# A sorted edge sum by matmul: one-hots of 128 columns, or two halves of a group with 64 columns each

## What is computed

```python
xn  = layernorm(x)
e   = edge_attr_128 @ W_edge + b_edge              # [50000, 256]
msg = relu(xn[src] + e)
agg = segment_sum(msg, dst, 3125)                  # dst is sorted
h   = (1 + eps) * xn + agg
h   = relu(h @ W1 + b1) @ W2 + b2                  # then batch norm and relu
x   = x + h + linear_attention(xn)                 # 8 heads, elu + 1
x   = x + moe(layernorm(x))                        # 8 experts, top 2
```

## Time and profile before

| | us |
|---|---|
| median of 3 runs | 1186.91 |
| span of the profiled execution (the page gives no other total) | 1050.8 |
| TensorE busy | 964.7 (92%) |
| weight loads busy | 810.3 (77%) |
| VectorE busy | 671.7 (64%) |
| POOL busy | 555.1 (53%) |
| ScalarE busy | 513.5 (49%) |

### The profile page before, as it was taken

One profiled execution on the slowest core, in us unless ns is written; L12 is line 12 of the kernel. 1 busy time (PEld: TensorE's weight loads), 2 busy tenths in 40 slices (PEclk: granted clock), 3 DMA queues, 4 the chain that ended last, 5 costly groups with the idle time before them and its releaser, 6 DMA issues.

```text
span 1050.8 us, 17977 instructions
## 1 busy us (share of the span) xinstructions
PE 964.7 (92%) x5112; PEld 810.3 (77%) x5113; DVE 671.7 (64%) x1274; ACT 513.5 (49%) x1036; POOL 555.1 (53%) x627
## 2 busy tenths in 40 slices
PE   5898999999999999999998961799999999999994
PEld 4677888888888888877775860778888888888884
DVE  5455565656655565578886778666666666666663
ACT  3644555555454545455554566444444444444442
POOL 3277777777777777777760040224253353444442
PEclk8899999999999999999998986899999999999998
DMA  9667788788888878998762028412545636635321
GB/s 246 197 154 237 255 267 253 250 268 266 260 254 262 269 247 267 278 313 270 239 202 86 26 89 316 181 26 40 204 90 174 220 50 213 192 73 160 98 38 21
DMA packets 85472, 198.30 MB, mean 189 GB/s; under 512 B 19785, under 2 KB 37139, under 8 KB 84378
## 3 DMA queue, kind: packets, MB, share of 16 engines
q1 hardware_dynamic: 55926, 131.60, 36.1%
q0 software_dynamic: 28752, 64.45, 25.5%
q10 hardware_dynamic: 724, 1.42, 0.5%
HBM read 147.86 MB, written 49.97 MB: 188 GB/s over the span
## 4 chain that ended last, share of the span: by engine, by line
POOL 29%; PE 29%; DMA 19%; issue 13%; DVE 7%; ACT 2%; POOLq 1%; SPq 0%; DVEq 0%; ACTq 0%
POOL work L758 29%; DMA out<-work,rowc 11%; PE banks L1141 6%; PE banks L1166 4%; DMA work<-token_table,tokc 4%; PE banks L470 3%; PE banks L446 3%; PE banks L1168 2%; PE banks L969 2%; PE banks L1054 2%; PE banks L1151 2%; DMA work<-in_edge_attr 1%; PE banks L1042 1%; DMA wts<-in_src 1%; DVE st L1776 1%
## 5 line engine op out<-in xcount | busy, mean ns | idle before, releaser
L758 POOL DMA_INDIRECT work<-node_table,srcT x391 | 379.5, 971 | 157.0 <-issue 117.6
L470 PE MATMUL banks<-work 128*128 128x256 f32 x780 | 179.1, 379 | 1.1 <-issue 1.1
L446 PE MATMUL banks<-w_edge,eaT 128*128 128x256 f32 x780 | 179.3, 380 | 0.0
L470 PEld LDWEIGHTS banks<-work 128*128 128x128 f32 x780 | 148.0, 190 | 21.8 <-issue 1.8
L446 PEld LDWEIGHTS banks<-w_edge,eaT 128*128 128x128 f32 x780 | 143.4, 191 | 16.8
L1166 PE MATMUL banks<-wsplit,hidT_hi 128*128 x416 | 153.3, 408 | 2.1 <-DVE hidT_lo L1908 2.1
L529 DVE TENSOR_TENSOR work<-banks,work 128x512 f32<-128x512 f32 x195 | 126.8, 682 | 26.1 <-DMA work<-node_table,srcT 15.2
L1141 PE MATMUL banks<-wsplit,xeT_hi 128*128 x416 | 134.3, 404 | 2.8 <-DVE xeT_lo L1915 2.8
L483 ACT COPY wts<-banks 128x256 f32<-128x256 f32 x66 | 24.6, 372 | 228.8 <-PE banks L470 227.8
L811 POOL DMA_INDIRECT out<-work,rowc x52 | 83.4, 1605 | 82.2 <-ACT work L1441 45.6
L1168 PE MATMUL banks<-wsplit,hidT_lo 128*128 x416 | 116.8, 281 | 0.0
(11 more groups left out here) (263 smaller groups left out, 1555.2 us busy)
## 6 DMA issues: line engine op xcount, KB each, us to landing
wsplit<-split_table SPq DMA_DIRECT2D x8, 4096.0 KB, 15.3
work<-in_edge_attr SPq DMA_DIRECT2D x65, 384.0 KB, 4.6
wts<-in_L_ffn_W SPq DMA_DIRECT2D x64, 256.0 KB, 4.9
split_table<-raw_hi SPq DMA_DIRECT2D x64, 256.0 KB, 3.0
split_table<-raw_lo SPq DMA_DIRECT2D x64, 256.0 KB, 4.3
work<-node_table,srcT POOLq DMA_INDIRECT x391, 4.2
xs<-in_x SPq DMA_DIRECT2D x8, 560.0 KB
wts<-in_L_ffn_b SPq DMA_DIRECT2D x8, 512.0 KB, 4.0
```

The costliest lines, as they stand in the source:

```text
L446: last = nc.tensor.matmul(b[:, k * DIM:(k + 1) * DIM], eaT[:, u, 2 * q + k], w_edge[:], start=True, stop=True)
L470: last = nc.tensor.matmul(bank[5][:, 0:DIM], onehot[:, u, j], msg[:, u, j], start=(j == 0), stop=(j == GT - 1))
L758: pool.indirect_dma_start(out=xg[n % NB][0:rows, j], out_offset=None, in_=node_table, in_offset=bass.IndirectOffsetOnAxis(ap=srcT[0:rows, ...
```

## The change

A group's 768 edges are split in two halves of 384. Each half has its own base node and a range of 64 nodes (`WINDOW = P // 2`). Edge rows lie so that tiles 0 to 2 of a partition belong to the first half and 3 to 5 to the second; `in_half` and `ids_of` deal them out in turn, so that the order of work takes a tile of the first half, then one of the second. A one-hot has 64 columns. The six matmuls write alternately to partitions 0 to 63 and 64 to 127 of bank 5, each half adding up its own three. After the copy and the turn, which stay as they were, VectorE adds the first 64 columns of each feature half at one offset (`add_first`, ahead of the one-hots) and the other 64 at a second (`add_second`, behind them). The second pass keeps its one-hots of 128 in functions of its own (left out here).

```diff
 PAIRS = GT // 2
+HALF = GROUP // 2
 PIECES = 4
 DEN0 = 2 * TILES + 1
 NB = 2
-WINDOW = P
-WINDOWS = -(-NODES // WINDOW)
+WINDOW = P // 2
+PASSES = -(-NODES // P)
...
+        onehot = view(work, 7680, 2, GT, WINDOW)
+        onehot_pass = view(work, 7680, GT, P)
 
...
-        numbers = bank[7][:, 3 * P:4 * P]
+        numbers = bank[7][:, 3 * P:3 * P + WINDOW]
...
-            rows = a["edge_attr_128"][bass.ds(g * GROUP, GROUP), :].rearrange("(p j) d -> p (j d)", j=GT)
-            sp.dma_start(ea[:, u].rearrange("p j d -> p (j d)"), rows).then_inc(ea_in[u], 16)
+            rows = a["edge_attr_128"][bass.ds(g * GROUP, GROUP), :].rearrange("(s p j) d -> p s (j d)", s=2, j=PAIRS)
+            sp.dma_start(ea[:, u].rearrange("p (s j) d -> p s (j d)", s=2), rows).then_inc(ea_in[u], 16)
...
+        def in_half(i):
+            return (i % 2) * PAIRS + i // 2
+        def ids_of(ids, i):
+            first = (i % 2) * HALF + i // 2
+            return ids[:, first:(i % 2 + 1) * HALF:PAIRS]
...
-                last = nc.tensor.transpose(bank[j // 3][:, (j % 3) * P:(j % 3 + 1) * P], ea[:, u, j], ident[:])
+                last = nc.tensor.transpose(bank[j // 3][:, (j % 3) * P:(j % 3 + 1) * P], ea[:, u, in_half(j)], ident[:])
...
-            nc.tensor.matmul(bank[5][:, 0:DIM], onehot[:, u, 0], msg[:, u, 0], start=True, stop=True).then_inc(agg_ready, 1)
+            for i in range(2):
+                last = nc.tensor.matmul(bank[5][i * WINDOW:(i + 1) * WINDOW, 0:DIM], onehot[:, u, i], msg[:, u, 0],
+                                        start=True, stop=True)
+            last.then_inc(agg_ready, 1)
...
-                last = nc.tensor.matmul(bank[5][:, 0:DIM], onehot[:, u, j], msg[:, u, j], start=(j == 0), stop=(j == GT - 1))
+                half = slice(j % 2 * WINDOW, (j % 2 + 1) * WINDOW)
+                last = nc.tensor.matmul(bank[5][half, 0:DIM], onehot[:, u, j], msg[:, u, j], start=(j < 2), stop=(j >= GT - 2))
+            last.then_inc(agg_ready, 1)
...
         def mark_from_psum(dve, g, u):
             dve.wait_ge(mx_ctx, g // 2)
-            nc.vector.tensor_tensor(onehot[:, u], numbers.unsqueeze(1).to_broadcast([P, GT, P]),
-                                    relT[:, g].unsqueeze(2).to_broadcast([P, GT, P]), ALU.is_equal).then_inc(onehot_ready, 1)
+            wide = [P, GT, WINDOW]
+            nc.vector.tensor_tensor(onehot[:, u], numbers.unsqueeze(1).to_broadcast(wide),
+                                    relT[:, g].unsqueeze(2).to_broadcast(wide), ALU.is_equal).then_inc(onehot_ready, 1)
 
         def mark_tail(dve, u):
-            nc.vector.tensor_scalar(onehot[:, u, 0], iota_f[:], relT[:, GROUPS - 1, 0:1], None, ALU.is_equal
+            wide = [P, 2, WINDOW]
+            nc.vector.tensor_tensor(onehot[:, u, 0:2], iota_f[:, 0:WINDOW].unsqueeze(1).to_broadcast(wide),
+                                    relT[:, GROUPS - 1, 0:2].unsqueeze(2).to_broadcast(wide), ALU.is_equal
                                     ).then_inc(onehot_ready, 1)
 
         def add_tail(dve, n, r, b, u):
...
+        turned = bank[5][:, DIM:2 * DIM].rearrange("p (h s c) -> p s h c", h=HALVES, s=2)
+        def add_first(dve, n, start, mixed, fresh=False):
             dve.wait_ge(agg_T, n + 1)
             if not fresh:
                 dve.wait_ge(agg_read, n)
             dve.wait_ge(mx_h, mixed)
             w = hT[:, :, bass.ds(start, WINDOW)]
+            nc.vector.tensor_tensor(w, turned[:, 0], w, ALU.add).then_inc(agg_first, 1)
...
+        def add_second(dve, n, start):
+            dve.wait_ge(agg_first, n + 1)
+            w = hT[:, :, bass.ds(start, WINDOW)]
+            nc.vector.tensor_tensor(w, turned[:, 1], w, ALU.add).then_inc(agg_read, 1)
...
-            nc.tensor.transpose(bank[6][0:1, 0:GROUPS], gstat[:, 0:1], ident[0:GROUPS, 0:GROUPS])
+            for i in range(2):
+                nc.tensor.transpose(bank[6][0:1, i * GROUPS:(i + 1) * GROUPS], gstat[:, i:i + 1], ident[0:GROUPS, 0:GROUPS])
             for j in range(GT):
-                nc.tensor.transpose(bank[4][:, j * GROUPS:(j + 1) * GROUPS], rel[:, j:GROUP:GT], ident[0:GROUPS, 0:GROUPS])
+                nc.tensor.transpose(bank[4][:, j * GROUPS:(j + 1) * GROUPS], ids_of(rel, j), ident[0:GROUPS, 0:GROUPS])
             nc.tensor.transpose(bank[4][:, GT * GROUPS:(GT + 1) * GROUPS], rel[:, 0:P], ident[0:GROUPS, 0:GROUPS])
             for j in range(GT):
...
-            step(nc.vector.tensor_reduce(gstat[:, 0:1], dst_f, AX.X, ALU.min))
-            step(nc.vector.tensor_scalar(gstat[:, 0:1], gstat[:, 0:1], 0.0, float(NODES - 1), ALU.max, ALU.min))
-            step(nc.vector.tensor_scalar(rel, dst_f, gstat[:, 0:1], None, ALU.subtract))
+            by_half_group = lambda v: v.rearrange("g (s e) -> g s e", s=2)
+            step(nc.vector.tensor_reduce(gstat[:, LOW], by_half_group(dst_f), AX.X, ALU.min))
+            step(nc.vector.tensor_scalar(gstat[:, LOW], gstat[:, LOW], 0.0, float(NODES - 1), ALU.max, ALU.min))
+            step(nc.vector.tensor_tensor(by_half_group(rel), by_half_group(dst_f),
+                                         gstat[:, LOW].unsqueeze(2).to_broadcast([GROUPS, 2, HALF]), ALU.subtract))
             step(nc.vector.tensor_copy(src_f, src_i))
...
             def windows_from(g):
-                return nc.values_load_multi_w_load_instructions(base_row[0:1, g:g + GT], engines=(DVE,), min_val=0,
+                return nc.values_load_multi_w_load_instructions(base_row[0:1, 2 * g:2 * (g + GT)], engines=(DVE,), min_val=0,
...
                 if n >= 2:
-                    add_window(dve, n - 2, starts[(n - 2) % GT], mixed_by(n + 1), n == 2)
+                    add_first(dve, n - 2, starts[2 * ((n - 2) % GT)], mixed_by(n + 1), n == 2)
                 if n >= 2:
                     dve.wait_ge(agg_ready, n - 1)
...
                     mark_from_psum(dve, n, n % 2)
+                if n >= 2:
+                    add_second(dve, n - 2, starts[2 * ((n - 2) % GT) + 1])
                 if n % 2 == 1 and n < 2 * TILES:
                     mix_k(n // 2)
...
```

More of the change, by code:

```diff
@@ L133, in build @@
         msg = view(work, 4608, 2, GT, DIM)
-        onehot = view(work, 7680, 2, GT, P)
+        onehot = view(work, 7680, 2, GT, WINDOW)
+        onehot_pass = view(work, 7680, GT, P)
         table_stage = view(work, 1536, STAGES * CHUNK_TILES, DIM).rearrange("p (u t) d -> p u t d", u=STAGES)
@@ L469, in aggregate, with aggregate_pass @@
                     pe.wait_ge(msg_ready, PAIRS * n + j // 2 + 1)
-                last = nc.tensor.matmul(bank[5][:, 0:DIM], onehot[:, u, j], msg[:, u, j], start=(j == 0), stop=(j == GT - 1))
+                half = slice(j % 2 * WINDOW, (j % 2 + 1) * WINDOW)
+                last = nc.tensor.matmul(bank[5][half, 0:DIM], onehot[:, u, j], msg[:, u, j], start=(j < 2), stop=(j >= GT - 2))
+            last.then_inc(agg_ready, 1)
+        def aggregate_pass(pe, n):
+            pe.wait_ge(agg_copied, n)
+            pe.wait_ge(agg_read, n)
+            pe.wait_ge(onehot_ready, n + 1)
+            pe.wait_ge(msg_ready, PAIRS * (n + 1))
+            for j in range(GT):
+                last = nc.tensor.matmul(bank[5][:, 0:DIM], onehot_pass[:, j], msg[:, 0, j], start=(j == 0), stop=(j == GT - 1))
             last.then_inc(agg_ready, 1)
@@ L659, in _ @@
             with sp.If(again > 0):
-                with sp.Fori(0, WINDOWS) as w:
+                with sp.Fori(0, PASSES) as w:
                     n0 = (w + 1) * GROUPS
@@ L763, in _ @@
             with pool.If(again > 0):
-                with pool.Fori(0, WINDOWS) as w:
+                with pool.Fori(0, PASSES) as w:
                     with pool.Fori(0, GROUPS) as g:
@@ L1335, in _ @@
             with act.If(again > 0):
-                with act.Fori(0, WINDOWS) as w:
+                with act.Fori(0, PASSES) as w:
                     with act.Fori(0, GROUPS) as g:
@@ L1557, in _ @@
                                                 op0=ALU.is_lt, op1=ALU.mult))
-            nc.vector.tensor_reduce(gstat[:, 1:2], span, AX.X, ALU.max).then_inc(top_ready, 1)
+            nc.vector.tensor_reduce(gstat[:, TOP], span, AX.X, ALU.max).then_inc(top_ready, 1)
             dve.wait_ge(top_T, 1)
-            step(nc.vector.tensor_reduce(gstat[0:1, 3:4], bank[6][0:1, 0:GROUPS], AX.X, ALU.max))
-            nc.vector.tensor_scalar(miss_i[:], gstat[0:1, 3:4], float(WINDOW), None, ALU.is_ge).then_inc(miss_known, 1)
+            step(nc.vector.tensor_reduce(gstat[0:1, MOST], bank[6][0:1, 0:GROUPS], AX.X, ALU.max))
+            nc.vector.tensor_scalar(miss_i[:], gstat[0:1, MOST], float(WINDOW), None, ALU.is_ge).then_inc(miss_known, 1)
             dve.wait_ge(miss_known, 1)
@@ L1661, in _ @@
             for n in range(GROUPS - 2, GROUPS):
-                add_window(dve, n, starts[n % GT], TILES)
+                add_first(dve, n, starts[2 * (n % GT)], TILES)
+                add_second(dve, n, starts[2 * (n % GT) + 1])
             round_low(dve, SPLITS - 1)
@@ L1681, in _ @@
```

(2 more changed lines are left out.)

47 lines of the change are left out of this document (29 added, 18 removed).

## The result

The changed kernel takes 1191.89 us, the median of 21 runs (1181.68 to 1214.13). The kernel before took 1180.17 us in 21 runs (1166.25 to 1190.77). The ratio is 1.0125, interval [1.0096, 1.0155]: slower by 12 to 15 us, where the forecast was 8 us faster. Ratios leave out executions more than 1.5% above a kernel's fastest, which cuts off the slow end of widely spread kernels (e17 keeps 5 of 12 executions, e5 3 of 6, e7 7 of 12, e4 8 of 14). The profiled execution of the changed kernel is its longest one (1214.13); a second one, in experiment e2, has the same stages and a span of 1215.5.

What follows compares the result with a forecast made beforehand. The prediction took POOL's gathers as the bound from 96 to 440 us, then DMA, then TensorE from 466 us; terms 0.4 - 1.8 - 1 + 1 - 4.6 + 1 - 3 = -8.0 us gave 1179 us, range 1167 to 1209.

Steps and rivals of the forecast that it cites:

- 96 to 440 us: First long stretch of the edge part: POOL's gathers bound it, so -1.8 us, and -1 for TensorE running ahead.
- POOL waiting for sums: Sign against the forecast: it is wrong if POOL waits for sums between 96 and 440 us.
- what surrounds the program: Outside the span: the 136.1 us between the 1050.8 us span and the 1186.91 us median, taken as untouched.
- Aggregation: A group's twelve matmul records on TensorE: 1.75 us instead of 2.59, bounds 1.51 and 2.59, saving 0.85 us per group.
- 466 to 546 us: Attention stretch, 9.6 groups: from TensorE's 8.31 us per group to POOL's 7.83, -4.6 us, bounds 0 and -7.7.
- 546 to 566 us: End of the edge part: TensorE finishes two aggregations faster and is no longer a group late, -3 us.
- Register loads: VectorE reads 12 window starts, not 6, every sixth group: 1.6 us more each, hidden in the first stretch, +1 later.
- 440 to 466 us: DMA-bound stretch: 128 more, smaller packets per group cost +1 us, bounds 0 and 4.
- Case E: Rival on edge-row DMA: the smaller packets starve the gathers, 1186 to 1205 us, chance 0.08.
- Case D: Rival around each aggregation: no overlap, array empties at whole/halved changes, 0.16 to 0.35 us each, 1208 to 1233 us, chance 0.19.
- C: Rival on the aggregation: the halves don't overlap and nothing else is lost, 1184 to 1188 us, chance 0.12.

Runs made afterwards that it cites:

- e17: The kernel before with the sums of features 128 to 255 left out of the aggregation, all 128 array columns kept: ratio 1.0054.
- e5: The changed kernel with tiles 0 to 2 and then 3 to 5 in place of in turn: ratio 1.0138.
- e7: The kernel before with one more unused matmul of 512 columns (4 instructions, 0.86 us) ahead of each aggregation: ratio 1.0092.
- e4: The changed kernel with one-hots 128 wide again and the aggregation on the whole array: ratio 1.0059.
- e2: The changed kernel once more, unchanged, against the kernel before: ratio 1.0158.
- e1: The kernel before once more, unchanged and profiled again: ratio 1.0025, profiled time 1179.18 us.
- e11: The changed kernel with the window starts loaded into VectorE's registers without bounds checks, against the kernel before: ratio 1.0090.
- e16: The changed kernel with one-hots 128 wide, whole-array aggregation and no bounds checks, against the kernel before: ratio 1.0005.
- e13: The kernel before with the load of six window starts made twice, 13 register instructions more each sixth group: ratio 1.0062.
- e3: The kernel before with only the edge rows in two runs of 1536 bytes per partition and the tiles dealt in turn: ratio 1.0017.
- e15: The changed kernel without bounds checks, with an unused matmul of 512 columns ahead of each aggregation, against the kernel before: ratio 1.0146.
- e8: The kernel before with six small unused matmuls (24 instructions, 0.38 us) ahead of each aggregation: ratio 1.0592.
- e9: The kernel before with the load of six window starts into VectorE's registers made four times: ratio 1.0564.

## Why the prediction was wrong

- **The step that failed** is in *96 to 440 us*, "POOL is the bound", with its basis "it has 2.05 us in hand and simply has no faster pace". It was true of the one execution on the page. In every other profile TensorE's signals come late, POOL waits for sums (142.7 us in e1) and two groups take 19.4 to 22.2 us, not 15.17. This is the sign that the prediction named against itself, POOL waiting for sums. The sum of the forecast, -8.0 us, also had no term for what less matmul work would cost; e11 against e16 puts the halved one-hots and aggregation at +0.85%, about 10 us, where 0.85 us less of TensorE's work a group stood as a gain.
- I could have seen it ahead of the result: I explained 136.1 us between span and median as "what surrounds the program". The runs' own spans lie only 1.7 us below their times. The 130 us were the difference between two kinds of execution.
- *Aggregation*: taken as 1.75, measured 1.44 to 1.52, the lower bound. The load was 140 ns (145 taken), the one-hot 548 (550), the adds 289 and 283 (284). The Trainium skill (TensorE: Matmul & The Clock Gate, Part 3) has the halves of the array run concurrently, and this trace agrees: 1.52 instead of 2.75 us, 1.8 times for two column tiles. The saving of 1.1 us a group bought nothing, since TensorE does not set the pace (e7) and its clock fell with less work: from 0.938 to 0.912 in e11 is 61 us more at 1.2 GHz (an estimate, 2 x 0.026 x 1180, as the lower level counts half in the mean).
- *466 to 546 us*, -4.6, and *546 to 566 us*, -3: both rested on TensorE as the bound there. In the changed kernel these groups lie at 588 to 707 us, and TensorE is busy 97 of these 119 us.
- *Register loads*: the 1.6 us more for each was right (1.4 measured). The cover was wrong: VectorE's 40% idle time does not hide it. e13 gives +7 us for such a dose, against the +1 of the sum. That VectorE's waits don't cover it because what it waits for is itself late is likely and not shown.
- *440 to 466 us*, the smaller packets: +1 taken, e3 shows none that can be measured. Case E is out.
- *Case D*, the drain: it is there, but small. Behind a whole-array record the first halved one starts 0.09 us later than usual (385.10 - 382.41 = 2.69 us instead of 2.59). Behind the aggregation it is the same: the last record starts 1.52 - 0.38 = 1.14 us after the first, the next work 1.44 after it, so 0.30 us apart instead of 0.22 (309 and 216 ns by the trace's starts). Two changes a group are 0.19 us, 12 us of TensorE's time in 65 groups; D had taken 0.16 to 0.35 for one. The rule of the Trainium skill (TensorEngine Tiling, Key Properties) that a change of tiling mode drains TensorE agrees with this trace, at 93 ns each. D named the right side, but its main premise, no overlap, was wrong, and no run takes the changes out alone.
- The measured 1191.89 lies in my range of 1167 to 1209 by luck: the range was wide for C, D and E, none of which happened as described, and the kernel before was itself 1180.17 in the runs beside it. In direction the forecast was wrong: faster by 8 us forecast, slower by 12 to 15 measured.

## What to carry over

Set the page's span against the times of the runs before reading anything from it: if they differ by more than a couple of microseconds, the page shows another kind of execution, and its bound may not be theirs. In a loop whose signals arrive late, time taken out of an engine is worth little, and added instructions cost (here about 45 ns each on TensorE beside the kernel before, about 25 beside the changed one): merging small instructions and leaving out bounds checks on clamped offsets is worth a try. Less matmul work between waits can also lower TensorE's granted clock and take back what it saved.

## What the runs showed of the hardware

- Signals of TensorE can be microseconds late (up to 12.4 us in the 60 groups of the changed kernel, 13.9 in e15) while its records go on at full pace and POOL, DMA and the other engines run. In e1 22 of 28 late copies start in a pause of POOL, though the pauses cover only 0.22 of the time. In the changed kernel it is 17 of 32 with 0.26, in e4 9 of 26 with 0.27; and a late signal makes POOL pause, so this says little of the cause. Behind the edge part, where no such gathers run, all kernels take 488 to 496 us, that of the page shown of before as well. What holds the signals is not shown.
- The trace of the page shown of before holds 17,102 semaphore events, those of the others 7,711 to 9,327 (7,822 in e1); up to 40 us they are alike (612 and 617 in e1), then from 40 to 560 us e1 has 2,736 where the page shown of before has 12,186. This is probably why they say "remote" or "another core" for waits on TensorE. Whether the recording of events and the late signals have one cause wasn't tried: every run here is recorded.
- Three matmuls on one half of the columns, then three on the other, take 2.00 us for twelve records (e5), between 1.52 in turn and 2.75 on the whole array.
- A change between the whole array and a half of its columns costs TensorE 93 ns: 309 ns from one record's start to the next instead of 216, on either side of the aggregation.
- The granted clock went with the matmul work in each group: 0.955 with a wide filler (e7), 0.938 without, 0.905 with half the features (e17). It went down as well where pauses grew: 0.925 in e8, 0.918 in e9.
